# A piecewise-linear gelu FFN stage: biases moved off TensorE, two sums moved from VectorE to GpSimd, two roundings moved from ScalarE to VectorE

## The reference, cut to what matters

```python
def float2fix(x, mantissa_bits):            # round to multiples of 2^-8
    s = jnp.float32(2.0 ** mantissa_bits)
    return x + (jnp.round(x * s) / s - x)
# x is layer-normalised over its 256 features
h = jnp.einsum('bsd,df->bsf', x, w1) + b1   # 256 -> 1024
h = float2fix(h, 8)
xq = float2fix(h, 8)                        # exact gelu at 33 knots 0.25 apart, straight lines between
y = jnp.interp(xq, _PWL_X, _PWL_Y)
y = jnp.where(xq > 4.0, xq, jnp.where(xq < -4.0, 0.0, y))
h = float2fix(float2fix(y, 8), 8)
out = jnp.einsum('bsf,fd->bsd', h, w2) + b2 # 1024 -> 256
x = x + float2fix(out, 8)
```

## Time and profile before

| what | value |
|---|---|
| median of three executions | 4531.46 us (4524.43 to 4533.0) |
| span of the profiled execution, first to last instruction | 4527.3 us |
| TensorE busy over the span | 3886.3 us (86%) |
| VectorE busy | 3074.1 us (68%) |
| ScalarE busy | 2057.9 us (45%) |
| GpSimd busy | 795.1 us (18%) |

### The profile page before, as it was taken

One profiled execution on the slowest core, in us unless ns is written; L12 is line 12 of the kernel. 1 busy time (PEld: TensorE's weight loads), 2 busy tenths in 40 slices (PEclk: granted clock), 3 DMA queues, 4 the chain that ended last, 5 costly groups with the idle time before them and its releaser, 6 DMA issues. The chain is left out here.

```text
span 4527.3 us, 83053 instructions
## 1 busy us (share of the span) xinstructions
PE 3886.3 (86%) x30431; PEld 2824.0 (62%) x30525; DVE 3074.1 (68%) x7110; ACT 2057.9 (45%) x3636; POOL 795.1 (18%) x510
## 2 busy tenths in 40 slices
PE   6799997799377999796399999779997987999899
PEld 5344443798365777575378888635555665555577
DVE  7666664456746666544566666678867887888587
ACT  3355554233103333342044444347775762777510
POOL 6433321401431000000023322410000013000000
PEclk9799999599668999897599999879998998999999
DMA  8233331201311000011054544722210015222000
GB/s 266 86 100 101 101 91 54 68 26 42 125 62 33 19 19 19 28 40 37 13 158 124 132 125 125 230 80 66 66 38 19 1 35 199 60 67 67 28 19 19
DMA packets 234478, 338.02 MB, mean 75 GB/s; under 512 B 39204, under 2 KB 132950, under 8 KB 234167
## 3 DMA queue, kind: packets, MB, share of 16 engines
q1 hardware_dynamic: 218280, 306.66, 21.4%
q0 software_dynamic: 15888, 27.23, 2.8%
HBM read 242.42 MB, written 107.01 MB: 77 GB/s over the span
## 5 line engine op out<-in xcount | busy, mean ns | idle before, releaser
L1918 ACT ACTIVATE a_pT<-a_psS 128x512 f32<-128x512 f32 x1536 | 836.0, 597 | 387.7 <-PE a_psS L1804 382.4
L1990 DVE TENSOR_REDUCE a_mx<-a_psA 128x1 f32<-128x512 f32 x1024 | 656.4, 685 | 82.9 <-PE a_psA L1782 82.8
L1819 PE MATMUL a_psZ<-a_pT,a_V 128*17 128x128 f32 x12288 | 488.8, 278 | 0.0
L1782 PE MATMUL a_psA<-a_ks,a_qs 48*128 48x512 f32 (+1 forms) x1536 | 405.5, 523 | 83.8 <-DVE a_mx L1990 36.9
L1986 DVE CUSTOM_DVE_ANT_0 a_scored<-a_psA,a_hide_q 128x512 bf16<-128x512 f32 x512 | 332.7, 688 | 184.4 <-PE a_psA L1782 183.3
L1819 PEld LDWEIGHTS a_psZ<-a_pT,a_V 128*17 128x17 f32 x12288 | 272.8, 97 | 272.7 <-issue 163.3
L1782 PEld LDWEIGHTS a_psA<-a_ks,a_qs 48*128 48x128 f32 (+1 forms) x1536 | 151.6, 192 | 330.2 <-DVE a_mx L1990 127.7
L1804 PE MATMUL a_psS<-a_qs,a_ks 50*128 50x512 f32 (+1 forms) x1536 | 318.3, 408 | 2.7 <-ACT a_pT L1918 0.8
L3262 DVE SCALAR_TENSOR_TENSOR ex_h<-ex_psU,ex_ub,ex_sg 128x512 f32<-128x512 f32 x129 | 96.9, 751 | 189.3 <-PE ex_psU L159 182.3
L2002 POOL TENSOR_TENSOR X<-X,a_osb 128x512 f32<-128x512 f32 x48 | 61.1, 1278 | 935.3 <-ACT a_osb L1905 917.3
L3208 ACT CAST ex_w_h<-X 128x1024 fp32r<-128x1024 f32 x102 | 106.0, 1040 | 149.5 <-DMA X<-in_L_ffn_gw 145.7
(11 more groups left out here) (606 smaller groups left out, 10227.2 us busy)
## 6 DMA issues: line engine op xcount, KB each, us to landing
a_qs<-a_q_parts SPq DMA_DIRECT2D x576, 64.0 KB, 2.3
a_ks<-a_k_parts SPq DMA_DIRECT2D x576, 64.0 KB, 2.3
a_k_parts<-a_p_kp SPq DMA_DIRECT2D x96, 256.0 KB, 2.6
a_q_parts<-a_p_qp SPq DMA_DIRECT2D x96, 256.0 KB, 3.2
X<-in_L_ffn_gw SPq DMA_DIRECT2D x36, 512.0 KB, 4.4
X<-in_L_ffn_up_w SPq DMA_DIRECT2D x36, 512.0 KB, 3.3
X<-in_L_ffn_down_w SPq DMA_DIRECT2D x36, 512.0 KB, 3.8
top_rows<-blank_rows SPq DMA_DIRECT2D x32, 514.0 KB, 4.8
```

The lines of the kernel that those rows point to most:

```text
L1782: nc.tensor.matmul(psA[:, unit(a, par) % 3], qs[r, g % ring, p % 2, q * P:(q + 1) * P], ks[r, g % ring, p % 2], start=True, stop=True).the ...
L1819: last = nc.tensor.matmul(psZ[q * VP:q * VP + VW, g % 2, j * P:(j + 1) * P], V[:, b, kt, g % NG * GH + j, :], pT[:, p % 2, par, kt, q * P: ...
L1918: nc.scalar.activation(pT[:, p % 2, par, kt, :], psS[:, unit(t, par) % 3], ACT.Exp).then_inc(exp_done, 1)
L1990: nc.vector.tensor_reduce(mx[:, p // 2 % 2, par, p % 2, q:q + 1], psA[:, unit(a, par) % 3], AX_X, ALU.max).then_inc(a_used, 1)
```

## The change

- b1 is loaded as eight rows and turned by one TensorE transposition into a column per slice, which is the bias operand of the ScalarE instruction that brings `psH` out (`biased`, tile `a`, no scaling). b2 is loaded into all partitions and added by VectorE as it takes `psY` (`take_outputs`). The short bias matmuls and the splitting of the biases into two rows go.
- Rounding is one VectorE instruction that adds a constant and subtracts it (`quantised`, tile `u`; `rounded`, tile `h`). ScalarE's `hR` and `h` go; VectorE's `scale_steps` becomes `quantised`.
- `fall` and `on_line` are done by GpSimd.
- All tiles between the steps are four deep, and the order on each engine is rewritten with up to three units ahead.
- At the end of a batch VectorE takes psY plus b2, ScalarE adds the rounding constant from SBUF (`rounded_outputs`), and VectorE subtracts it and adds to `X` in one instruction (`add_outputs`).
- Moments are taken for 8 token tiles ahead of everything and for the other 24 within units 0 to 5, four tiles each.

```diff
-        rounder, unrounder, knot0, knot1 = (sb(n, [P, 1]) for n in ("rounder", "unrounder", "knot0", "knot1"))
-        uR, w, cR, fr = sb("uR", [P, 2, S]), sb("w", [P, 2, S]), sb("cR", [P, 2, S]), sb("fr", [P, 4, S])
-        g0, g1, drop, line, hR = (sb(n, [P, 2, S]) for n in ("g0", "g1", "drop", "line", "hR"))
-        h = sb("h", [P, 2, S])
+        b1_rows, b1, b2 = sb("b1_rows", [MF, P]), sb("b1", [P, MF]), sb("b2", [P, D])
+        a, u, cR, fr, g0, g1, drop, line, h = (sb(n, [P, DEEP, S]) for n in ("a", "u", "cR", "fr", "g0", "g1", "drop", "line", "h"))
...
+                def fall(n):
+                    pool.wait_ge(g_ready, n + 1)
+                    if n >= DEEP:
+                        pool.wait_ge(t_ready, n - DEEP + 1)
+                    nc.gpsimd.tensor_tensor(drop[:, n % DEEP], g0[:, n % DEEP], g1[:, n % DEEP], ALU.subtract).then_inc(drop_ready, 1)
+
+                def on_line(n):
+                    pool.wait_ge(t_ready, n + 1)
+                    if n >= DEEP:
+                        pool.wait_ge(h_ready, n - DEEP + 1)
+                    nc.gpsimd.tensor_tensor(line[:, n % DEEP], fr[:, n % DEEP], g0[:, n % DEEP], ALU.add).then_inc(line_ready, 1)
+
+                fall(0)
+                on_line(0)
+                fall(1)
+                for n in range(UNITS):
+                    if n + 1 < UNITS:
+                        on_line(n + 1)
+                    if n + 2 < UNITS:
+                        fall(n + 2)
...
-                    nc.scalar.activation(uR[:, n % 2, :], psH[:, n % AHEAD, :], ACT.Identity, bias=rounder[:], scale=Q).then_inc(u_ready, 1)
+                    nc.scalar.activation(a[:, n % DEEP], psH[:, n % AHEAD, :], ACT.Identity, bias=b1[:, m:m + 1]).then_inc(a_ready, 1)
...
                 for n in range(UNITS):
                     m = n % MF
-                    if n + 1 < UNITS:
-                        gelus(n + 1)
+                    if n + 3 < UNITS:
+                        biased(n + 3)
+                    if n + 2 < UNITS:
+                        gelus(n + 2)
                     if m == 0 and n > 0:
-                        outputs(n // MF - 1)
-                    act.wait_ge(line_ready, n + 1)
-                    nc.scalar.activation(hR[:, n % 2, :], line[:, n % 2, :], ACT.Identity, bias=rounder[:], scale=Q).then_inc(hR_ready, 1)
...
-                    nc.scalar.activation(h[:, n % 2, :], hR[:, n % 2, :], ACT.Identity, bias=unrounder[:], scale=1 / Q).then_inc(h_ready, 1)
-                    if m == 2 and n // MF + 1 < B:
+                        rounded_outputs(n // MF - 1)
+                    if m == 1 and n // MF + 1 < B:
                         high(n // MF + 1)
...
+                def quantised(n):
+                    dve.wait_ge(a_ready, n + 1)
+                    if n >= DEEP:
+                        dve.wait_ge(fr_ready, n - DEEP + 1)
+                    nc.vector.tensor_scalar(u[:, n % DEEP], a[:, n % DEEP], ROUND_FINE, ROUND_FINE, ALU.add, ALU.subtract).then_inc(u_ready, 1)
...
-                    nc.vector.tensor_tensor(fr[:, n % 4, :], fr[:, n % 4, :], drop[:, n % 2, :], ALU.mult).then_inc(t_ready, 1)
+                    nc.vector.scalar_tensor_tensor(fr[:, n % DEEP], fr[:, n % DEEP], 1 / KNOT, drop[:, n % DEEP], ALU.mult,
+                                                   ALU.mult).then_inc(t_ready, 1)
+
+                def rounded(n):
+                    dve.wait_ge(line_ready, n + 1)
+                    if n >= DEEP:
+                        dve.wait_ge(h_used, n - DEEP + 1)
+                    nc.vector.tensor_scalar(h[:, n % DEEP], line[:, n % DEEP], ROUND_FINE, ROUND_FINE, ALU.add, ALU.subtract).then_inc(h_ready, 1)
+
+                def take_outputs(b):
+                    dve.wait_ge(h_used, (b + 1) * MF)
+                    if b > 0:
+                        dve.wait_ge(y_rounded, b)
+                    nc.vector.tensor_tensor(y[:], psY[:], b2[:].unsqueeze(1).to_broadcast([P, TB, D]), ALU.add).then_inc(y_taken, 1)
+
+                def add_outputs(b):
+                    dve.wait_ge(y_rounded, b + 1)
                     tiles = G.X[:, b * TB:(b + 1) * TB, :]
-                    nc.vector.tensor_tensor(tiles, tiles, yR[:], ALU.add).then_inc(x_added, 1)
...
+                    nc.vector.scalar_tensor_tensor(tiles, yR[:], ROUND_FINE, tiles, ALU.subtract, ALU.add).then_inc(x_added, 1)
...
                 for n in range(UNITS):
                     m, b = n % MF, n // MF
-                    fall(n)
-                    if n + 2 < UNITS:
-                        scale_steps(n + 2)
-                    slope(n)
-                    if n + 2 < UNITS:
-                        round_knot(n + 2)
-                    on_line(n)
-                    if n + 2 < UNITS:
-                        fraction(n + 2)
+                    rounded(n)
+                    if m == 0 and b > 0:
+                        take_outputs(b - 1)
+                    if n + 3 < UNITS:
+                        quantised(n + 3)
+                    if n + 1 < UNITS:
+                        slope(n + 1)
+                    if n + 3 < UNITS:
+                        round_knot(n + 3)
                     if m == 0 and b + 1 < B:
+                        if b == 1:
+                            inverse(1, slice(EARLY, TILES))
                         normalise(b + 1)
+                    if n + 3 < UNITS:
+                        fraction(n + 3)
+                    if n < MF - 2:
+                        moments(range(EARLY + n * late, EARLY + (n + 1) * late))
+                    if n == MF - 2:
+                        variances(slice(EARLY, TILES))
                     if m == 1 and b > 0:
-                        tail(b - 1)
+                        add_outputs(b - 1)
                     if m == 2 and b + 1 < B:
                         low(b + 1)
```

More of the change, by code:

```diff
@@ L1122, in turn @@
                     last.then_inc(xT_in_psum, 1)
[L1124 to L1129, removed]
                 def hidden(n):
@@ L1142, in down @@
                     if m == 0 and n > 0:
-                        pe.wait_ge(y_free, n // MF)
+                        pe.wait_ge(y_taken, n // MF)
                     for t in range(TB):
[L1145 to L1148, removed]
+                        last = nc.tensor.matmul(psY[:, t, :], h[:, n % DEEP, t * P:(t + 1) * P], w2[:, m, :], start=(m == 0 and t % 2 == 0),
                                                 stop=(m == MF - 1), skip_group_check=True)
@@ L1227, in _, with moments, variances @@
                         high(n // MF + 1)
-                outputs(B - 1)
+                    if n == MF - 1:
+                        root(1, slice(EARLY, TILES))
+                rounded_outputs(B - 1)
             @block.vector
             def _(dve):
+                link = chained(dve, norm_chain)
+                def moments(tiles):
+                    for k in tiles:
+                        last = nc.vector.bn_stats(stats[:, k, :], G.X[:, k, :])
+                    link(last)
+                def variances(cols):
+                    nc.vector.tensor_tensor(diff[:, cols], stats[:, cols, 1], stats[:, cols, 4], ALU.subtract)
+                    nc.vector.tensor_tensor(within[:, cols], stats[:, cols, 2], stats[:, cols, 5], ALU.add)
+                    link(nc.vector.tensor_tensor(total[:, cols], stats[:, cols, 1], stats[:, cols, 4], ALU.add))
+                    nc.vector.scalar_tensor_tensor(between[:, cols], diff[:, cols], 0.25, diff[:, cols], ALU.mult, ALU.mult)
+                    nc.vector.tensor_scalar(mean[:, cols], total[:, cols], 0.5, None, ALU.mult)
+                    link(nc.vector.tensor_scalar(within[:, cols], within[:, cols], 1.0 / D, LN_EPS, ALU.mult, ALU.add))
+                    nc.vector.tensor_tensor(var[:, cols], within[:, cols], between[:, cols], ALU.add).then_inc(var_ready, 1)
@@ L1285, in _ @@
-                link = chained(dve, norm_chain)
-                for k in range(TILES):
-                    last = nc.vector.bn_stats(stats[:, k, :], G.X[:, k, :])
-                link(last)
-                nc.vector.tensor_tensor(diff[:], stats[:, :, 1], stats[:, :, 4], ALU.subtract)
-                nc.vector.tensor_tensor(within[:], stats[:, :, 2], stats[:, :, 5], ALU.add)
-                link(nc.vector.tensor_tensor(total[:], stats[:, :, 1], stats[:, :, 4], ALU.add))
-                nc.vector.scalar_tensor_tensor(between[:], diff[:], 0.25, diff[:], ALU.mult, ALU.mult)
@@ L1293, in _ @@
-                nc.vector.tensor_scalar(mean[:], total[:], 0.5, None, ALU.mult)
-                link(nc.vector.tensor_scalar(within[:], within[:], 1.0 / D, LN_EPS, ALU.mult, ALU.add))
-                nc.vector.tensor_tensor(var[:], within[:], between[:], ALU.add).then_inc(var_ready, 1)
-                dve.wait_ge(row_high, 1)
-                nc.vector.tensor_tensor(row_l[:], row[:], b12[0:1].bitcast(F32), ALU.subtract).then_inc(row_low, 1)
-                dve.wait_ge(std_ready, 1)
```

(3 more changed lines are left out.)

134 lines of the change are left out of this document (64 added, 70 removed).

## The result

The changed kernel takes 4555.21 us (median of seven executions, 4543.21 to 4568.09), beside 4530.45 for the kernel before (seven, 4524.43 to 4539.78). The ratio is 1.0049, with a 95% interval of 1.0034 to 1.0064: slower by half a per cent, some 25 us. The forecast was 4563 in a range of 4512 to 4600.

The account below looks back on a forecast made before the run. VectorE and GpSimd taking turns at a shared port were to set the unit: 63 x 4.42 plus 25, plus 4, minus 3 = 304.5 us against 265.0, start -8, together +31.5 on 4531.5: 4563 us, range 4512 to 4600.

Parts of the forecast that it names:

- The unit: One plain unit of the stage: five VectorE instructions taking turns with two GpSimd sums at the SBUF port, 4.42 us.
- `round_knot` with `on_line`: Within a unit: `on_line` on GpSimd waits for `round_knot`, and `fraction` comes after it; 1.43 us together.
- `fraction` with `fall`: Within a unit: `fraction` goes ahead of GpSimd's waiting `fall`, and `rounded` comes after it; 1.70 us together.
- Once per batch: VectorE work beside the units: `normalise` 1.3, `add_outputs` 1.14, `take_outputs` 1.14, `low` nothing; 3.6 us per batch, 25 for seven.
- Once: One-time terms: start -8 us from fewer moments ahead, moved moments +4, last three units -3, end even.
- The moved moments: Moments moved into the first units: about 0.3 us in six units, variance steps some 2; +4 us, between 0 and 8.
- the last three units: Units without `quantised`, `round_knot` or `fraction`, to run at about 3.35 us each; -3 us.
- The port not felt: Rival, chance 0.08: VectorE and GpSimd work at once, so a unit takes 3.35 us; 4479 us in all.
- Only two-input instructions held: Rival, chance 0.08: `rounded`, `quantised` and `round_knot` run under GpSimd, 3.80 us per unit; some 4514 us.
- No overlap: Rival, chance 0.06: each turn at the port costs both full durations, 5.23 us per unit; 4614 us.
- where the four buffers don't absorb that: Clock rival, chance 0.15: TensorE at 1.2 GHz falls behind; unabsorbed, up to 5 us per batch, 4598 us.
- the ring: `fall`, `slope`, `on_line` wait on each other between GpSimd and VectorE; 3.35 us per unit without blocking, not opened by deeper buffers.

Follow-up runs that it names:

- moments_ahead: The changed kernel with the moments of all 32 tiles taken ahead again, as before the change; 4564.39 us in one execution.
- gpsimd_writes_only: The changed kernel with GpSimd's two sums replaced by constant fills of the same tiles, so the sums are left out; 4458.74 us in one execution.
- one_sum: The changed kernel with `on_line` back on VectorE and `fall` still on GpSimd; 4524.0 us in one execution.
- three_deep: The changed kernel with all tiles three deep instead of four; 4555.41 us in one execution.
- sums_vector: The changed kernel with both sums (`fall`, `on_line`) back on VectorE, all else as changed; 4500.33 us, ratio 0.9945 to the kernel before.
- vector_scalar_balance: `sums_vector` with b2 put on TensorE, and ScalarE rounding straight from `psY` and normalising; 4509.77 us, ratio 0.9962 to the kernel before.

## Why the prediction was right

The mechanism and nearly every term of the sum held.

**The unit.** Predicted 4.42, measured 4.37 (63 steps: -3 us). By its parts, taking a held instruction to begin its own length before its end: `slope` 0.60 (0.61 predicted); `round_knot` with `on_line`, 3550.58 to 3552.00, 1.42 (1.43); `fraction` with `fall`, to 3553.68, 1.68 (1.70); `rounded` 0.33 (0.34); `quantised` 0.34 (0.34). The overlaps are 0.13 to 0.15 us at each hand-over, as read from rows 7 of the second attention stage.

**Once per batch.** A regular batch is 38.34 us, so 38.34 - 8 x 4.37 = 3.38 us beside its units, predicted 3.6: `take_outputs` and `add_outputs` 1.14 each, as predicted; `normalise` 1.03 net instead of 1.3, as `fraction` and `rounded` behind it aren't held; `low` 0.05, hidden as it was said to be.

**Once.** From the start of the stage to the first `h`, 23.2 us against 32.7 to the first `hR` before: -9.5, predicted -8. First to last `h`, 302.4 (3439.1 to 3741.5), predicted 304.5. The moved moments were mis-sized: `moments_ahead` puts them at 5.2 us, predicted 4 with bounds of 0 and 8. Of the last three units only two are short (3.46 and 3.45 us, predicted 3.35; the one ahead of them takes 4.35): -1.9, predicted -3. So 63 x 4.37 + 7 x 3.38 + 5.2 - 1.9 = 302.3. The end was called even and is 1.0 longer (7.7 us behind the last `h` against 6.7 behind the last `hR`). Together 302.4 - 265.0 - 9.5 + 1.0 = 28.9 in the trace, as the stage has it; predicted 31.5, and the medians differ by 25.

**Readings that were off.** The batch of 33.14 us is an average with the shorter last one; a regular batch of the kernel before is 34.04 us, which the sum doesn't use. Units of 4.2 to 4.65 us give 4549 to 4577, not 4548 to 4580. And `on_line`, forecast at 1.7 to 2 us, takes 1.40, as it is issued only 0.26 us before `round_knot` ends; the sum goes by the ends and is not touched by it.

**The rivals.** The port not felt asked for 3.35 us per unit and 0.43 and 0.69 for the VectorE forms; they take up to 1.65. Only two-input instructions held: `rounded` at 1.49 contradicts it, and `gpsimd_writes_only` shows that the two kinds are held by different things. No overlap: 5.23 per unit against 4.37. The rule of the Trainium skill (SBUF — State Buffer, "Who interferes with whom") that the loser is blocked for the whole instruction is 0.27 us per turn too strict here; `one_sum` shows that the first to be issued isn't always let in first. The clock did fall from 2.4 to 1.2 GHz at times: its mean was 0.61 from 3560 to 3564, after TensorE had stood 2.2 us for `take_outputs`, and 0.91 to 1.00 over regular batches. Two of these, from first `h` to first `h`, and the end of the stage:

```profile
3595.38:3633.72 38.34, 27.86 (x122) 21.34 (x121) 38.10 (x48) 18.02 (x26) 24.20 (x17) 1.00 0.00 1
...
3672.08:3710.44 38.36, 30.10 (x122) 23.29 (x121) 38.12 (x49) 17.91 (x26) 24.23 (x17) 0.91 0.00 1
...
3740.00:3744.00 4.00, 4.00 (x11) 3.11 (x11) 0.50 (x2) 0.00 (x0) 1.26 (x1) 0.50 0.00 0
```

A batch takes 38.34 us at 1.00 and 38.36 at 0.91, with VectorE busy throughout: the buffers took it up. That step of the rival, "where the four buffers don't absorb that", is the one that failed; with three buffers (`three_deep`) the stage is no longer either. Only the end pays: VectorE waits 3.6 us there for the last `psY`, and 2.1 in `moments_ahead`, whose clock there, from 3738 to 3740, was 1.00. That is 1.5 us, and without it the end would be 0.5 shorter than before and not 1.0 longer. A clock well below 1, named in the prediction as a sign of being wrong, was seen in stretches and cost no more than that.

**What was said to be worth nothing.** The bias matmuls and ScalarE's two roundings were costed at nothing under the ring, with a gain if that cover went. `sums_vector` comes nearest to that case, 4500 us, but its gain of 30 us holds the deeper buffers, the new order and the moved moments as well; what these two edits give alone was not measured.

## What to carry to other kernels

Before work is moved from VectorE to an idle GpSimd, reckon what VectorE loses: here each GpSimd sum of 1.28 us took 1.08 us from VectorE to spare it 0.61 (the unit of 4.37 us, less the 3.42 - 2 x 0.61 = 2.20 of VectorE's other five instructions, is 2.17 for two). The idle engine was no free engine; the Trainium skill's caution that moving work between these two might not help (Perfetto Trace Analysis, "Optimizing Scalar/DVE Operations") was what happened. If a sum must be there, put it under VectorE instructions with an operand in PSUM: they are slower by themselves (0.69 against 0.41) and still saved 49 us against the same order with `u` in SBUF, 30 against the changed kernel, though VectorE alone was better by another 25 (4500 against 4525).

A change of many parts is best taken apart: this one held a gain of 21 to 30 us and a loss of 50 to 55 (by the stage and by the medians). And the fallen clock was dear only where TensorE had little to spare: it cost nothing per batch in the changed kernel, where TensorE was busy 27.86 of 38.34 us at full clock, and 3.1 us in `vector_scalar_balance`, where it was 29.74 of 30.16.

## What was not expected of the hardware

- VectorE can starve GpSimd. In `one_sum` a GpSimd sum issued at 3587.22 ended 4.04 us later, one at 3675.40 took 5.16, and the longest, at 3469.77, 7.13, while VectorE ran instruction after instruction at full speed; in other units of the same kernel it was let in after 0.3 us. In the changed kernel no sum of the stage took over 1.75 us.
- A GpSimd fill holds a one-input VectorE instruction (560 ns against 411) and not a two-input one (692 at the median, 694 at most); a GpSimd sum holds both.
